# One PSUM bank for projections, low-rank stage, transposes and keys, worked in bursts, and a third bank for the exponentials' scores

## The reference

```python
def attn(x, wq, wk, wv, wo):            # x: 2 x 2048 x 1024, 32 heads of 32
    q, k, v = (x @ wq).reshape(B, T, 32, 32), x @ wk, x @ wv
    scores = einsum('bqhd,bkd->bhqk', q, k) / sqrt(32)
    probs = softmax(where(causal, scores, -inf))
    return einsum('bhqk,bkd->bqhd', probs, v).reshape(B, T, C) @ wo

def ffn(x, A, B, Wr, br):               # A: 8 x 16 x 1024, B: 8 x 1024 x 16
    scores = 8 * softmax(x @ Wr.T + br)
    low = einsum('bsd,hrd->bshr', x, A)
    return 2 * einsum('bshr,hor,bsh->bso', low, B, scores)

x = x + layernorm(attn(layernorm(x), ...))
x = x + layernorm(ffn(layernorm(x), ...))
```

## Time and profile before

| | |
|---|---|
| median of 3 runs | 3832.42 us (3829.83 to 3839.87) |
| the profiled execution | 3834.05 us |
| its span, first to last instruction | 3832.3 us |
| granted TensorE clock over the span | 0.965 |
| PE busy | 3486.2 us, 91% |
| DVE busy | 2486.3 us, 65% |
| POOL busy | 1931.8 us, 50% |
| ACT busy | 1584.8 us, 41% |

### The profile page before, as it was taken

How to read it: one execution, slowest core, us unless ns; L and a number is a source line. 1 busy time by engine, 2 the same in 40 slices (tenths; PEclk the granted TensorE clock), 3 DMA queues, 4 the chain that set the end, 5 groups by cost and what they waited for, 6 DMA issues and landing times.

```text
span 3832.3 us, 47700 instructions
## 1 busy us (share of the span) xinstructions
PE 3486.2 (91%) x17496; PEld 1672.1 (44%) x17496; DVE 2486.3 (65%) x5584; ACT 1584.8 (41%) x3089; POOL 1931.8 (50%) x510
## 2 busy tenths in 40 slices
PE   5799989999999999899998999889999899999984
PEld 3444444444444444444344444444444444444432
DVE  3566786667766666774367677776676756667424
ACT  0233434444444444445433343444444444445541
POOL 0224455545454666656612354565354565667750
PEclk8899999999999999999999999999999999999996
DMA  3312101110110100000121211110100101100000
GB/s 78 118 45 70 45 31 34 56 34 26 32 27 24 52 20 26 25 20 20 56 59 45 70 39 50 34 56 26 39 26 23 32 20 28 32 20 15 18 1 33
DMA packets 132330, 144.19 MB, mean 38 GB/s; under 512 B 28024, under 2 KB 93560, under 8 KB 132096
## 3 DMA queue, kind: packets, MB, share of 16 engines
q1 hardware_dynamic: 132096, 141.13, 12.6%
HBM read 72.91 MB, written 16.78 MB: 23 GB/s over the span
## 4 chain that ended last, share of the span: by engine, by line
PE 70%; DVE 17%; POOL 5%; ACT 3%; issue 2%; SPq 2%; DMA 1%; POOLq 0%; ACTq 0%; DVEq 0%
PE ps L964 13%; PE ps L978 13%; PE ps L993 12%; PE ps L950 10%; PE ps L1100 9%; DVE mx L712 6%; POOL ds L506 4%; DVE ps L729 2%; PE ps L1002 2%; PE ps L1051 2%; PE ps L1142 2%; PE ps L1024 2%; SPq L407 1%; PE ps L967 1%; PE ps L1130 1%
## 5 line engine op out<-in xcount | busy, mean ns | idle before, releaser
L712 DVE TENSOR_REDUCE mx<-ps 128x1 f32<-128x512 f32 (+3 forms) x2560 | 1492.0, 602 | 943.6 <-PE ps L967 473.8
L547 ACT ACTIVATE pr<-ps 128x512 f32<-128x512 f32 (+3 forms) x2560 | 1320.3, 534 | 1603.1 <-PE ps L981 834.7
L506 POOL TENSOR_TENSOR ds<-ds,pr 128x2048 f32<-128x2048 f32 (+3 forms) x384 | 1570.6, 4090 | 494.7 <-ACT pr L547 469.3
L978 PE MATMUL ps<-qs,ks 98*128 98x512 f32 (+3 forms) x2560 | 1354.7, 533 | 46.0 <-ACT pr L547 33.2
L964 PE MATMUL ps<-ks,qs 96*128 96x512 f32 (+3 forms) x2560 | 1043.4, 414 | 168.3 <-DVE mx L712 135.6
L978 PEld LDWEIGHTS ps<-qs,ks 98*128 98x128 f32 x2560 | 492.6, 193 | 747.5 <-ACT pr L547 443.7
L503 POOL TENSOR_TENSOR ds<-pr 128x2048 f32<-128x2048 f32 (+1 forms) x64 | 273.4, 4272 | 957.3 <-ACT pr L547 957.3
L964 PEld LDWEIGHTS ps<-ks,qs 96*128 96x128 f32 x2560 | 503.3, 198 | 351.5 <-DVE mx L712 247.8
L993 PE MATMUL ps<-pr,vs 128*32 128x512 f32 (+3 forms) x5120 | 615.4, 553 | 0.0
L950 PE MATMUL ps<-xT,wq_sb 128*128 128x512 f32 x1024 | 547.7, 619 | 13.9 <-DVE ks L778 12.5
L1100 PE MATMUL ps<-wo_sb,ao 128*128 128x512 f32 x928 | 486.8, 608 | 2.6 <-DVE zs L755 1.4
(11 more groups left out here) (123 smaller groups left out, 2015.7 us busy)
## 6 DMA issues: line engine op xcount, KB each, us to landing
qs<-q SPq DMA_DIRECT2D x768, 64.0 KB, 2.0
wq_sb<-in_L_attn_wq_dram SPq DMA_DIRECT2D x64, 512.0 KB, 3.9
t<-in_L_attn_x_dram SPq DMA_DIRECT2D x32, 512.0 KB, 6.8
xr<-in_L_attn_x_dram SPq DMA_DIRECT2D x32, 512.0 KB, 3.5
out_dram<-xr SPq DMA_DIRECT2D x32, 512.0 KB, 2.7
qs<-mT SPq DMA_DIRECT2D x256, 4.0 KB
wo_sb<-in_L_attn_wo_dram SPq DMA_DIRECT2D x1, 4096.0 KB, 13.7
zs<-in_L_ffn_A_dram SPq DMA_DIRECT2D x1, 512.0 KB
```

The lines of the kernel that those rows point to most:

```text
L506: nc.gpsimd.tensor_tensor(ds[:, :, c0:], ds[:, :, c0:], this, ALU.add).then_inc(added, 1)
L547: nc.scalar.activation(pr[:, k % NS, g, c0:], ps[:, PST + g % 2, c0:], ACT.Exp, scale=SCALE).then_inc(exp_done, 1)
L712: nc.vector.tensor_reduce(mx[:, qt * GH + g, c_:c_ + 1], ps[:, PM + g % 2, 0:w], AX.X, ALU.max).then_inc(mx_done, 1)
L978: last = nc.tensor.matmul(ps[:, bank, c0:], ks[0:STK + 2, c:c + P], qs[0:STK + 2, n % NS, g, c0:], start=True, stop=not diagonal)
```

## The change

`PQ` and `PO` become one bank `PX`, and the bank that comes free makes `PST` three banks, used in turn by the running number of the score; the wait is for the exponential three back. Since all pieces now use one bank one after the other, `bank_left` knows every kind of piece and waits for the copy of whichever had it before. The tables are rewritten so that the products of a piece stand close together (1.5 of 64 apart and not 4), and the pieces one behind the other: the first half of a projection at 48 to 58 of a unit, the low-rank stage at 0 to 14 of the unit after the next, the second half of the projection at 18 to 28, the queries at 32 to 42, the keys at 17 to 27 of unit 5. The low-rank stage of a block's last tile moves from unit 6 to unit 5, the transposes `tr` from the start of unit 5 to the end of unit 4, and the normalizations before them 12 places ahead. The first block's transposes, ahead of the loop, take all eight banks in turn.

```diff
-        for m, first in ((2, 0), (3, 32)) if n == 0 else ((n + 3, 32),):
+        for m, first in ((2, 0), (3, 32)) if n == 0 else ((n + 3, 44 if u == 5 and N == 16 else 32),):
             if m < UN:
+                apart = 3 if blk or u == 4 else 4 if u == 5 else 7
                 for k in range(KT):
-                    at(64 * u + first + 4 * k, "PE", "q", m, k)
-                for who in ("ACT", "DVE", "SP"):
-                    at(64 * u + first + 4 * (KT - 1), who, "q", m)
-        if blk == 0 and u == 2:
+                    at(64 * u + first + apart * k // 2, "PE", "q", m, k)
+                for who in ("ACT", "DVE"):
+                    at(64 * u + first + apart * 7 // 2 + 1, who, "q", m)
+                at(64 * u + (first + 25 if m == n + 2 else 63), "SP", "q", m)
...
+        if blk == 0:
             for i in range(5):
-                put(3 * i, "PE", "wt", i)
-                put(3 * i, "DVE", "wt", i)
+                at(64 * 2 + 5 * i, "PE", "wt", i)
+                at(64 * 2 + 5 * i, "DVE", "wt", i)
...
-            j, t0 = blk * TB + i, 64 * i + 32
-            at(t0 + 16, "SP", "residual", j)
-            for h in range(2):
+            j = blk * TB + i
+            at(64 * i + 40, "SP", "residual", j)
+            for h, t0 in ((0, 64 * i + 48), (1, 64 * i + 82)):
                 for k in range(KT):
-                    at(t0 + 32 * h + 4 * k, "PE", "proj", j, h, k)
-                at(t0 + 32 * h + 28, "ACT", "proj", j, h)
-            at(t0 + 34, "DVE", "att", j, 0)
-            for k in range(1, 14):
-                at(t0 + 62 + 2 * k, "DVE", "att", j, k)
-            lora(at, t0 + 96 if i < TB - 1 else 64 * 6, j)
+                    at(t0 + 3 * k // 2, "PE", "proj", j, h, k)
+                at(t0 + 11, "ACT", "proj", j, h)
+                at(t0 + 14, "DVE", "att", j, h)
+            for k in range(2, 14):
+                at(64 * i + 96 + 2 * k, "DVE", "att", j, k)
+            lora(at, 64 * i + 128, j)
...
         for h in range(2):
-            at(t0 + 1 + 4 * h, "PE", "turn", j, h)
-            at(t0 + 1 + 4 * h, "ACT", "turn", j, h)
-        at(t0 + 9, "PE", "low", j)
-        at(t0 + 9, "ACT", "low", j)
-        at(t0 + 9, "DVE", "low", j, 0)
-        at(t0 + 13, "DVE", "low", j, 1)
-        at(t0 + 16, "PE", "slt", j)
-        at(t0 + 16, "ACT", "slt", j)
+            at(t0 + 3 * h, "PE", "turn", j, h)
+            at(t0 + 3 * h, "ACT", "turn", j, h)
+        for who, *part in (("PE",), ("ACT",), ("DVE", 0)):
+            at(t0 + 6, who, "low", j, *part)
+        at(t0 + 8, "DVE", "low", j, 1)
+        at(t0 + 10, "PE", "slt", j)
+        at(t0 + 10, "ACT", "slt", j)
         for h in range(2):
             for who in ("PE", "ACT", "DVE"):
-                at(t0 + 20 + 4 * h, who, "up", j, h)
+                at(t0 + 12 + 2 * h, who, "up", j, h)
         for c in range(4):
-            at(t0 + 26 + 2 * c, "DVE", "up", j, 2 + c)
-        at(t0 + 36, "ACT", "out", j)
-        at(t0 + 38, "POOL", "out", j)
-        at(t0 + 44, "SP", "store", j)
+            at(t0 + 16 + 2 * c, "DVE", "up", j, 2 + c)
+        at(t0 + 26, "ACT", "out", j)
+        at(t0 + 28, "POOL", "out", j)
+        at(t0 + 34, "SP", "store", j)
...
-            at(64 * 4 + 24 + 8 * i, "DVE", "norm", blk, i)
-            for h in range(2):
-                at(64 * 5 + 4 * i + 2 * h, "PE", "tr", blk, i, h)
-            at(64 * 5 + 4 * i, "ACT", "tr", blk, i)
-            at(64 * 5 + 4 * i + 2, "DVE", "tr", blk, i)
+            at(64 * 4 + 12 + 8 * i, "DVE", "norm", blk, i)
+            for h, who in enumerate(("ACT", "DVE")):
+                at(64 * 4 + 48 + 4 * i + 2 * h, "PE", "tr", blk, i, h)
+                at(64 * 4 + 48 + 4 * i + 2 * h, who, "tr", blk, i)
         for k in range(KT):
-            at(64 * 5 + 16 + 2 * k, "PE", "kv", blk, k)
-        at(64 * 5 + 30, "ACT", "kv", blk)
-        at(64 * 5 + 30, "DVE", "kv", blk)
+            at(64 * 5 + 17 + 3 * k // 2, "PE", "kv", blk, k)
+        at(64 * 5 + 28, "ACT", "kv", blk)
+        at(64 * 5 + 28, "DVE", "kv", blk)
...
-        PM, PST, PPV, PQ, PO, PAUX = 0, 2, 4, 5, 6, 7
+        NPM, NPS = 2, 3
+        PM, PST, PPV, PX, PAUX = 0, 2, 5, 6, 7
...
-        def projections_bank():
-
+            order = [("kv", 0), ("q", 0), ("q", 1)]
...
-                        if stage == "tr" and a[2] == 0:
-                            order.append(("tr", a[0] * TB + a[1]))
+                        if stage == "tr":
+                            order.append(("tr", 2 * (a[0] * TB + a[1]) + a[2]))
                         elif stage in ("kv", "q") and a[1] == 0:
                             order.append((stage, a[0]))
                         elif stage == "turn" and a[1] == 0:
                             order.append(("lora", a[0]))
+                        elif stage in ("proj", "early") and a[2] == 0:
+                            order.append((stage, 2 * a[0] + a[1]))
+                        elif stage == "wt":
+                            order.append(("wt", a[0]))
             order += [("lora", LAST * TB + i) for i in range(TB)]
-            return dict(zip(order, [(None, 0)] + order))
-
-        PQ_BEFORE = projections_bank()
+            return dict(zip(order, [("", 0)] + order))
+
+        BEFORE = shared_bank()
...
+        def turn_bank(j, h):
+            return (2 * j + h) if j < TB else PX
+
         def proj_bank(j, h):
-            return PM + h if j >= LAST * TB else PO
+            return PM + h if j >= LAST * TB else PX
...
-                before, y = PQ_BEFORE[kind, x]
+                before, y = BEFORE[kind, x]
...
                 elif before == "tr":
-                    pe.wait_ge(xt_act, y + 1)
+                    pe.wait_ge((xt_act, xt_dve)[y % 2], y // 2 + 1)
                 elif before == "lora":
                     pe.wait_ge(y2_sb, 2 * (y + 1))
+                elif before == "proj":
+                    pe.wait_ge(z1_ready, y + 1)
+                elif before == "early":
+                    pe.wait_ge(early_sb, y + 1)
+                elif before == "wt":
+                    pe.wait_ge(wt_done, y + 1)
...
-                if k >= 2:
-                    pe.wait_ge(mx_done, k - 1)
-                bank, c = PM + g % 2, key_slot(n, c) * BLK
+                if k >= NPM:
+                    pe.wait_ge(mx_done, k - NPM + 1)
+                bank, c = PM + k % NPM, key_slot(n, c) * BLK
...
-                if k >= 2:
-                    pe.wait_ge(exp_done, k - 1)
-                bank, c = PST + g % 2, key_slot(n, t // TB) * BLK + t % TB * P
+                if k >= NPS:
+                    pe.wait_ge(exp_done, k - NPS + 1)
+                bank, c = PST + k % NPS, key_slot(n, t // TB) * BLK + t % TB * P
...
-                if h == 0:
-                    bank_left("tr", j)
-                elif j:
-                    pe.wait_ge(xt_dve, j)
-                if i == 0 and blk >= 2 and h == 1:
-                    pe.wait_ge(z1_ready, 2 * TB * (blk - 1))
-                if i == 0 and blk == 1 and h == 1:
-                    pe.wait_ge(wt_done, 5)
+                if blk:
+                    bank_left("tr", 2 * j + h)
...
-                    last = nc.tensor.transpose(ps[:, (PQ, PO)[h], k * P:(k + 1) * P], t4[:, i, kk * P:(kk + 1) * P], ident[:, :])
+                    last = nc.tensor.transpose(ps[:, turn_bank(j, h), k * P:(k + 1) * P], t4[:, i, kk * P:(kk + 1) * P], ident[:, :])
...
-                    if j % TB == 0 and h == 0 and j < LAST * TB:
-                        pe.wait_ge(xt_dve, j + TB)
-                    if j >= LAST * TB:
-                        if j % TB:
-                            pe.wait_ge(z1_ready, 2 * j + h - 1)
-                    elif j or h:
-                        pe.wait_ge(z1_ready, 2 * j + h)
+                    if j < LAST * TB:
+                        bank_left("proj", 2 * j + h)
+                    elif j % TB:
+                        pe.wait_ge(z1_ready, 2 * j + h - 1)
...
-                if k == 0 and i == 0 and h == 0:
-                    pe.wait_ge(ao_ready, LAST * NU + EARLY)
-                    pe.wait_ge(z1_ready, 2 * TB * LAST)
-                elif k == 0:
-                    pe.wait_ge(early_sb, 2 * i + h)
-                last = nc.tensor.matmul(ps[:, PO, :], ao[:, (LAST * NU + k) % NAO, i * P:(i + 1) * P],
+                if k == 0:
+                    bank_left("early", 2 * i + h)
+                    if i == 0 and h == 0:
+                        pe.wait_ge(ao_ready, LAST * NU + EARLY)
+                last = nc.tensor.matmul(ps[:, PX, :], ao[:, (LAST * NU + k) % NAO, i * P:(i + 1) * P],
```

64 lines of the change are left out of this document (31 added, 33 removed).

## The result

The changed kernel takes 3954.39 us (median of 4 runs, 3948.93 to 3959.48) against 3835.13 us for the kernel before beside it: 1.0311 times as long, 95% interval 1.0296 to 1.0327. The forecast was 3814 with a range up to 3852, so the time lies 140 us above the forecast and outside the range, on the other side.

What follows compares the result with a forecast made beforehand. It took TensorE's waits to bound the kernel: 135.6 us for VectorE's maxima, 33.2 for ScalarE's exponentials. Terms -20 -21 +16 +9 +10 -6 -8 = -20 took 3834 to 3814 us, range 3771 to 3852.

Steps and rivals of the forecast that it cites:

- Part 1: Third bank for the exponentials' scores: shorter waits for exponentials and fewer late weight loads, -20 us, ends 0 and 65.
- Part 2: Query and key bursts that end early: waits for their copies go, bursts cost nothing in the array, -21 us.
- Part 3: One shared bank: copy waits in 16-slot low-rank stages, +16 us (4.7 a tile), and in the next block's transposes, +9.
- Part 4: What stands where: bunched projections +10 us, the fourth tile's low-rank stage moved -6, normalizations moved ahead -8.
- loss of cover: Projection's second half bunched into one quarter of a unit covers less waiting: +10 us, at most 24.
- moved low-rank stage: Fourth tile's low-rank stage goes from unit 6 to unit 5, beside the keys' products: -6 us, ends 0 and -16.
- normalizations: Next block's four normalizations 12 slots earlier, away from the finished tile's layer norm: -8 us, ends +5 and -20.
- Rival 1: TensorE passes the exponential and stands at the next maxima product; third bank and normalizations give nothing: 3842 us, chance 0.26.
- Rival 2: Shared-bank hand-overs bind everywhere; 24 low-rank stages outside the 16-slot blocks pay 4.7 us too: 3908 us, chance 0.17.
- Rival 3: Late weight loads count fully and half-speed stretches go with the gaps; third bank gives 65 us: 3769 us, chance 0.10.
- the rule on rotating banks: Independent matmul groups should rotate through PSUM banks: against folding two banks into one, for the third score bank; no separate size.

Runs made afterwards that it cites:

- e9: Kernel before with the small weight step folded, normalizations on ScalarE, and the residual made by ScalarE and GpSimd except in the last four tiles: 3748.3 us, 0.9765.
- e3: Changed kernel with the third bank off, two banks for the exponentials' scores as before: 3995.4 us, 1.0420.
- e10: Kernel before, banks untouched, with only the eight query products bunched, 1.5 slots apart and not 4: 3880.7 us, 1.0112.
- e5: Changed kernel's placement on the banks of the kernel before, two shared banks and two for the exponentials: 3958.4 us, 1.0317.
- e11: Kernel before, banks untouched, with only each half of a token tile's projection bunched in one burst: 3921.7 us, 1.0221.
- e8: Kernel before with the small weight step folded and the next block's normalizations on ScalarE: 3758.6 us, 0.9797.
- e7: Changed kernel with three moves undone (fourth tile's low-rank stage in unit 6, transposes in unit 5, normalizations 12 slots later): 3956.8 us, 1.0313.
- e15: Changed kernel with small weight step folded, late queries spread, normalizations on ScalarE, and projection's first half spread over slots 44 to 58: 3814.5 us, 0.9940.
- e16: e15 with the moves of the fourth tile's low-rank stage, the transposes and the normalizations also undone, as in e7: 3836.9 us, 0.9999.
- e17: e9 plus the change's moves of low-rank stage, transposes and normalizations, on its own banks, with the queries of unit 4 bunched: 3760.8 us, 0.9800.
- e2: Changed kernel with the small VectorE weight step (128x8) folded into the product behind it and ScalarE's copy: 3900.8 us, 1.0184.
- e4: Kernel before with the small VectorE weight step folded away in the same manner as e2: 3791.6 us, 0.9888.

## Why the prediction was wrong

**What bounds the kernel.** I read the waits and took the one for the maxima as VectorE's own load. It was right that TensorE stands for VectorE; but the cause of a late maximum is often one step ahead of it in VectorE's queue that stands for GpSimd: with these steps moved (e9) half of the wait is gone. The row was there, among VectorE's groups by shape of the kernel before (busy us, mean ns), and I had not looked for a small step with a large mean:

```profile
L841 DVE TENSOR_SCALAR lw<-le,lr 128x8 f32<-128x8 f32 x32 | 39.5, 1235 | 1.1
```

**Part 1** (-20): right in kind, too small: 41 us (e3). The visible wait halved, as I had taken it, but two thirds of that came back as waits for the maxima, and only 6 us less standing were left. The gain lay in the late loads, 20 us by the count of the earlier trace rows where I took a few, and some 8 in the clock.

**Part 2** is the step that failed: "Bursts as such save no time in the array" and "Nothing is late next there". It put the price of bunching at nothing. The waits it named did go. But the spread products were the work that TensorE had while VectorE caught up: bunching the queries costs 45 us (e10), for a wait of 10.4 us saved, and with the projections (part 4, below) it comes to 131 where the sum had +10. I priced a placement by the products' own length and their hand-overs, and not by what stands still beside them.

**Part 3** (+16 +9) was right in its standing. The four waits of a low-rank stage came to 4.5 us where I had 4.7 (waits of TensorE in unit 34 of the changed kernel):

```profile
PE ps L1137 <- DVE sl L851: 1.5, 1, 1.5
PE ps L1144 <- ACT zs L602: 1.4, 1, 1.4
PE ps L1103 <- ACT zs L602: 0.8, 1, 0.8
PE ps L1126 <- ACT hT L589: 0.8, 1, 0.8
```

The transposes of the next block wait 11.6 us for their copies in the whole loop where I had 9. But I put all of it down to the one bank, and of the four only that of the projection (1103) does; the other three come with two shared banks as well (e5). The fold itself costs 37 us (e5 to e3). That this lies within my ends (10 to 46) is luck: nearly all of it is clock, which I had at nothing, and in the profiled executions 20 us of it fall in the blocks with 32 slots, where I had next to nothing.

**Part 4**: the loss of cover (+10, ends 0 and 24) was the right mechanism, mis-sized: bunching the projections cost 86 us (e11). The 2.6 us that I read as the price of the products in a half unit with 64 slots was itself misread, since unit 24 ran at a granted clock of 0.89 and unit 25 at 1.00. In e8 both run at full speed (first halves of units 24 and 25, same order of columns):

```profile
1222.70:1252.42 29.72, 28.84 (x162) 12.74 (x160) 21.32 (x38) 17.81 (x33) 20.48 (x5) 1.00 0.36 115
1295.49:1330.11 34.62, 34.38 (x177) 15.74 (x177) 22.52 (x39) 18.94 (x35) 23.93 (x6) 1.00 0.15 39
```

The price is 4.9 us there. So my 24 us rested on a cover of 3.9 us that is only 1.6 by these rows, and the 86 us came otherwise: in e11 TensorE stands 47 us longer and half of the half-speed time is 37 us more. The moved low-rank stage (-6) and normalizations (-8) came to nothing on the changed kernel (e7), -22 on the repaired one (e15, e16), +12 on the repaired kernel before (e17). Unit 28 came 2.7 us nearer to unit 27 (100.8 against 92.7 us, 99.7 against 88.9 before), but only since unit 27 became longer.

**The rivals.** Rival 1 had the wait right and the time wrong: the maxima took over 12.4 of the 17.9 us that the exponentials lost (e3), and the third bank still gave 41 us. Rival 2 named a right place, the low-rank stages outside the 16-slot block, and the slower side, and put 3908 on it. But of its 24 stages the eight with 64 slots stand 2.47 us each at `slt`, the eight with 48 slots 1.6 on average at the up-product, and those with 32 slots at neither, some 33 us against its 94. Its cause, the hand-over of the bank, is not the one for the 2.47 us: folding one held step away takes the stop with the bank unchanged (e2). Rival 3's idea that the gaps decide the clock was right with its sign turned: I had it only as an upside. The layouts that I weighed by the rule on rotating banks differ by 37 us (the fold) and 41 us (the third bank), which cancel.

**The range** left the clock out on its slow side, though with the earlier trace rows at 0.88 and 0.91 I had seen that stops and half speed go together. All its terms there were standing time. Even with every term at its slow end (0, -21, +28, +18, +24, 0, +5) the sum gives 3888 us, 66 short of the measured time.

## What to carry to other kernels

Independent products spread thinly over a loop are cover for the engine that is behind; before bunching them, ask in each slot what TensorE has left to do while the slower engine clears its backlog, and price a new stop at its length plus half of the half-speed time that follows. Look for small instructions with a large mean duration on VectorE while GpSimd works: such a step is worth moving to another engine, or into a read from PSUM, as e4, e8 and e9 show (44, 33 and 10 us). Take an edit that changes banks and placement apart before judging it: here the third bank gave 41 us, the fold took 37 and the placement 123.

## What the chip showed beyond that

A stop of 1.75 us was followed by 20.5 us at half speed (unit 38) and one of 0.93 us by another 20.5 (unit 46, from 2605), while several stops of 2.4 and 2.5 us (units 9, 10, 17, 18) were followed by none; standing plus half of the half-speed time explains the spans of the table to some 20 us apart from the third bank's share (some 25), but which stop is followed by a fall stays open. The hold between VectorE and GpSimd is exact: the rest of the add plus 1.08 to 1.09 us for 128x1024 with two inputs, plus 0.55 for 128x1024 with one, plus 0.03 for 128x8. No step that reads PSUM, no reduction and no one-element step took over 0.01 us longer beside an add than without.
